# Flamingo block in fp32 on one core: weight centring and scaling moved from GpSimd to VectorE, keys and values taken ahead of the maxima

## The reference

```
x = x + tanh(g_xattn) * attention(layernorm(x), ctx)
x = x + tanh(g_ffn)   * experts(layernorm(x))

attention:  ln = LN(h); xq_t = fp8(clip(ln / in_scale_t))           t in q, qx, k, v
            q, qx, k = LN over D of ((xq_t * in_scale_t) @ W_t.T * w_scale_t), v likewise without LN
            kx, vx = split(ctx @ w_kv_x.T); kx = LN over D
            core = softmax(q k / sqrt(D)) v;  xout = softmax(qx kx / sqrt(D)) vx
            out = fp8(clip(cat(core, xout) / smooth)) @ wproj.T * scales
experts:    8 experts, top 2 of softmax(30 tanh(x @ w_gate / 30)), h = silu(x @ w1) * (x @ w3), out = h @ w2
```

## Time and profile before

| what | value |
| --- | --- |
| device time, median of 3 runs | 826.39 us |
| device time of the profiled execution | 827.05 us |
| its span, first to last instruction | 825.0 us |
| granted TensorE clock, mean | 0.96 |
| busy: PE, DVE, ACT, POOL | 84%, 62%, 61%, 60% |
| busy of a unit of the last group (16.76 us): PE, DVE, ACT, POOL | 16.03, 12.28, 13.48, 10.49 us |

### The profile page before, as it was taken

How to read it: one execution, slowest core, us unless ns; L and a number is a source line. 1 busy time by engine, 2 the same in 40 slices (tenths; PEclk the granted TensorE clock), 3 DMA queues, 4 the chain that set the end, 5 groups by cost and what they waited for, 6 DMA issues and landing times. The chain is left out here.

```text
span 825.0 us, 14882 instructions
## 1 busy us (share of the span) xinstructions
PE 691.2 (84%) x4662; PEld 593.5 (72%) x4663; DVE 512.5 (62%) x1148; ACT 502.0 (61%) x1861; POOL 495.2 (60%) x681
## 2 busy tenths in 40 slices
PE   0278899899989899998999998999875559999992
PEld 0267788888888888888888887889864426565662
DVE  5976767877777787777777767777776341211210
ACT  1567786887787788778778787778751112222220
POOL 4347687768867776886777687676542023444332
PEclk9999999999999999999999999999998559999997
DMA  5010110010010001001000100100000867532223
GB/s 183 27 51 1 40 39 1 1 53 27 1 52 27 1 2 52 26 1 52 27 1 2 52 26 2 52 2 1 1 1 2 269 191 248 131 51 41 48 32 70
DMA packets 35924, 38.90 MB, mean 47 GB/s; under 512 B 2720, under 2 KB 30752, under 8 KB 35840
## 3 DMA queue, kind: packets, MB, share of 16 engines
q1 hardware_dynamic: 31440, 32.02, 12.2%
q0 software_dynamic: 4416, 6.03, 4.5%
HBM read 32.67 MB, written 6.42 MB: 47 GB/s over the span
## 5 line engine op out<-in xcount | busy, mean ns | idle before, releaser
L796 POOL TENSOR_SCALAR probs<-probs,rsum 128x256 f32<-128x256 f32 x256 | 154.4, 614 | 75.9 <-DVE rsum L578 72.2
L405 ACT ACTIVATE probs<-s,nmax 128x256 f32<-128x256 f32 x256 | 122.0, 497 | 1.6 <-DVE nmax L573 1.6
L411 ACT CAST pt_hi<-t 128x512 fp32r<-128x512 f32 x128 | 75.8, 592 | 71.2 <-PE t L260 71.1
L419 ACT ACTIVATE qk<-t,head_w 128x512 f32<-128x512 f32 (+1 forms) x128 | 83.6, 682 | 45.3 <-PE t L272 45.3
L583 DVE TENSOR_TENSOR pt_lo<-t,pt_hi 128x512 fp32r<-128x512 f32 x128 | 87.6, 684 | 32.1 <-ACT pt_hi L411 31.7
L260 PE MATMUL t<-ident,probs 128*128 128x128 f32 x512 | 78.3, 275 | 17.3 <-POOL probs L796 16.5
L790 POOL TENSOR_TENSOR rstd<-rstd,half 128x6 f32<-128x6 f32 x64 | 87.7, 1371 | 5.3
L214 PE MATMUL pj_a<-w_ring,xq 128*128 128x256 f32 x496 | 75.0, 294 | 17.7 <-DVE w_ring L632 15.2
L573 DVE TENSOR_REDUCE nmax<-s 128x2 f32<-128x512 f32 x128 | 86.8, 679 | 0.0
L226 PE MATMUL pj_b<-w_ring,xq 128*128 128x128 f32 x496 | 68.9, 282 | 20.2 <-DVE v_lo L556 20.2
L1085 PE MATMUL h<-w_sb,xsT 128*128 x184 | 84.7, 604 | 0.6 <-ACT xsT L1192 0.5
(11 more groups left out here) (190 smaller groups left out, 1796.9 us busy)
## 6 DMA issues: line engine op xcount, KB each, us to landing
w_sb<-in_w SPq DMA_DIRECT2D x24, 512.0 KB, 5.2
spare<-in_wT SPq DMA_DIRECT2D x16, 256.0 KB, 2.9
wp_raw<-in_wpT SPq DMA_DIRECT2D x16, 256.0 KB, 2.9
spare<-in_wT SPq DMA_DIRECT2D x16, 128.0 KB, 3.1
spare<-in_wkvT SPq DMA_DIRECT2D x16, 128.0 KB, 3.1
acc<-in_x SPq DMA_DIRECT2D x1, 1024.0 KB, 5.9
start<-in_ctxT SPq DMA_DIRECT2D x1, 1024.0 KB, 7.2
spare<-in_x SPq DMA_DIRECT2D x1, 1024.0 KB, 5.4
```

The lines of the kernel that those rows point to most:

```text
L405: e = act.activation(probs[:, st, h * S:(h + 1) * S], s_bank[st][:, h * S:(h + 1) * S], ACT.Exp, bias=nmax[:, st, h:h + 1], accum_out=psum ...
L411: act.copy(pt_hi[:, :, st * P:(st + 1) * P], pt_bank[:].rearrange("p (n s) -> p n s", n=4)).then_inc(pthi_done, 1)
L419: m = act.activation(qk[:, at + c0:at + c0 + n], hd_bank[:, c0:c0 + n], ACT.Identity, scale=head_w[:, 2 * w:2 * w + 1], bias=head_w[:, 2 * ...
L796: m = pool.tensor_scalar(probs[:, st, c], probs[:, st, c], rsum[:, st, h:h + 1], 1.0, ALU.mult, ALU.mult)
```

## The change

POOL no longer scales and centres weights; DVE does both. The product of input scale and weight scale is written once into `w_scale`. `sum_weights(g, k)` now takes one half k, straight from the loaded weights, and makes the mean. `centre_weights(g, k, blocks)` subtracts the mean and multiplies by the scale in one small instruction for each block of 128 columns, 7 a half and 14 a group. They are spread over units: the sums of group g + 2 in b = 2 (one half at the start of the unit, one in its middle), the blocks of half 0 in b = 3 and those of half 1 in the b = 0 that follows (four at the start, three in the middle). For group 1 the sums and blocks lie in unit 0. ACT's casts and DVE's weights_lo lie in b = 0 and b = 1. `wp_hi` and `wp_lo` are cut in two halves, in b = 2 and b = 3. In the second half of a unit DVE takes normalise_kv(u+2, 0) ahead of both row_max, and quantise(u-1, 1) behind probs_lo.

```diff
@@ -437,8 +440,7 @@
 
-                if c % 2 == 0:
-                    act.wait_ge(w_centred, 2 * g + 1 + c // 2)
+                act.wait_ge(w_centred, 2 * g + 1 + c // 2)
                 if c == 0:
@@ -489,28 +491,33 @@
 
+            def prepare(g, b, place):
+
+                if g + 1 < G and b < 2:
+                    c = 2 * b + place if g > 0 else (b - 1) * 9 + 2 * place
+                    for n in ((c,) if g > 0 else (c, c + 1)):
+                        if 0 <= n < 4:
+                            weights_hi(g + 1, (g + 1) % 2, n)
+
             def step(g, par, b):
...
                 g1 = later(g, par, b, -1)[0]
-                prep = b == 1 and below(u + 4)
 
...
                     probs_hi(u - 1, 1, 0)
+                prepare(g, b, 0)
                 if below(u + 1):
...
                 exps(u, 0, 0)
-                if prep:
-                    weights_hi(g + 1, 1 - par, 0)
                 if above(u, 0):
...
                 exps(u, 0, 1)
-                if prep:
-                    weights_hi(g + 1, 1 - par, 1)
+                prepare(g, b, 1)
                 if above(u, 0):
@@ -518,15 +525,11 @@
                 probs_hi(u, 0, 1)
-                if prep:
-                    weights_hi(g + 1, 1 - par, 2)
                 exps(u, 1, 0)
...
                 exps(u, 1, 1)
-                if prep:
-                    weights_hi(g + 1, 1 - par, 3)
                 smooth(g, u, 0)
@@ -621,10 +624,24 @@
 
-            def sum_weights(g):
-                dve.wait_ge(w_scaled, g + 1)
-                dve.tensor_reduce(w_mean[:], w_raw[:, :, 0:NC_C * D].rearrange("p k (n d) -> p k n d", d=D), AX,
+            def sum_weights(g, k):
+                dve.wait_ge(w_loaded, 16 * W_DMAS * (g + 1))
+                dve.tensor_reduce(w_sum[:, k], w_raw[:, k, 0:NC_C * D].rearrange("p (n d) -> p n d", d=D), AX,
                                   ALU.add).then_inc(w_summed, 1)
+                dve.wait_ge(w_summed, KT * g + k + 1)
+                dve.tensor_scalar(w_mean[:, k], w_sum[:, k], 1.0 / D, None, ALU.mult).then_inc(w_meaned, 1)
+
+            def centre_weights(g, k, blocks):
+
+                dve.wait_ge(w_meaned, KT * g + k + 1)
+                for n in blocks:
+                    w = w_raw[:, k, n * D:(n + 1) * D]
+                    if n < NC_C:
+                        m = dve.tensor_scalar(w, w, w_mean[:, k, n:n + 1], w_scale[:, k, n:n + 1], ALU.subtract, ALU.mult)
+                    else:
+                        m = dve.tensor_scalar(w, w, w_scale[:, k, n:n + 1], None, ALU.mult)
+                if n == 7:
+                    m.then_inc(w_centred, 1)
 
@@ -635,6 +652,7 @@
             dve.memset(half[:], -0.5)
+            dve.memset(w_scale[:], 1.0).then_inc(ones_set, 1)
             dve.wait_ge(x_loaded, 16)
@@ -651,13 +669,22 @@
             dve.tensor_scalar(inv_smooth[:], inv_smooth[:], GRID, None, ALU.mult).then_inc(consts_ready, 1)
+            dve.wait_ge(ones_set, 1)
+            for i, blks in enumerate(((0, 1), (2, 3), (4,), (7,))):
+                for n in blks:
+                    m = dve.tensor_tensor(w_scale[:, :, n], col[:, C_INS + i * KT:C_INS + (i + 1) * KT],
+                                          col[:, C_SCAL + i:C_SCAL + i + 1].broadcast_to([P, KT]), ALU.mult)
+            m.then_inc(w_scales_ready, 1)
             dve.wait_ge(ctx_hi_done, 1)
...
                                   ALU.subtract, ALU.mult).then_inc(z_ready, 1)
-            sum_weights(0)
+            dve.wait_ge(w_scales_ready, 1)
+            for k in range(KT):
+                sum_weights(0, k)
+                centre_weights(0, k, (0, 1, 2, 3, 4, 5, 7))
             dve.wait_ge(consts_ready, 1)
@@ -705,11 +732,24 @@
 
+            def prepare(g, b, place):
+
+                if g == 0 and b == 0:
+                    centre_weights(1, place, (0, 1, 2, 3, 4, 5, 7))
+                if b == 2 and g + 2 < G:
+                    sum_weights(g + 2, place)
+                if b == 3 and g + 2 < G:
+                    centre_weights(g + 2, 0, ((0, 1, 2, 3), (4, 5, 7))[place])
+                if b == 0 and g > 0 and g + 1 < G:
+                    centre_weights(g + 1, 1, ((0, 1, 2, 3), (4, 5, 7))[place])
+
             def step(g, par, b):
...
                 bv, bh = (b + 2) % B, (b + 1) % B
-                prep = b == 1 and below(u + 4)
-
+                if u == 0:
+                    for k in range(KT):
+                        sum_weights(1, k)
+                prepare(g, b, 0)
                 if above(u, 0):
@@ -727,21 +767,22 @@
                     split_heads(u + 1, bh, 0)
-                if prep:
-                    weights_lo(g + 1, 1 - par, 0)
-                    weights_lo(g + 1, 1 - par, 1)
+                if g + 1 < G and b == 1:
+                    for c in ((0, 1) if g == 0 else (2,)):
+                        weights_lo(g + 1, 1 - par, c)
                 row_sum(u, 0, 1)
 
+                prepare(g, b, 1)
                 if below(u + 2):
...
                 probs_lo(u, 0, 0)
+                if below(u + 2):
+                    normalise_kv(u + 2, bv, 0)
                 row_max(u, 1, 0)
+                row_max(u, 1, 1)
+                probs_lo(u, 0, 1)
                 if above(u, 0):
                     quantise(u - 1, 1)
-                if below(u + 2):
-                    normalise_kv(u + 2, bv, 0)
-                row_max(u, 1, 1)
-                probs_lo(u, 0, 1)
                 row_sum(u, 1, 0)
@@ -749,13 +790,14 @@
                             x1_normalise(b - 3)
-                if b == 0 and below(u + 4):
-                    sum_weights(g + 1)
                 if below(u + 1):
                     split_heads(u + 1, bh, 1)
-                if prep:
-                    weights_lo(g + 1, 1 - par, 2)
-                    weights_lo(g + 1, 1 - par, 3)
+                if g + 1 < G and g > 0 and b == 0:
+                    for c in (0, 1):
+                        weights_lo(g + 1, 1 - par, c)
+                if g + 1 < G and b == 1:
+                    for c in ((2, 3) if g == 0 else (3,)):
+                        weights_lo(g + 1, 1 - par, c)
                 row_sum(u, 1, 1)
@@ -818,36 +860,22 @@
 
-            def scale_weights(g):
-
-                wait(w_loaded, 16 * W_DMAS * (g + 1))
-                for i, (blk, n) in enumerate(((0, 2), (2, 2), (4, 1), (7, 1))):
-                    for k in range(KT):
-                        w = w_raw[:, k, blk * D:(blk + n) * D]
-                        m = pool.tensor_scalar(w, w, col[:, C_INS + i * KT + k:C_INS + i * KT + k + 1],
-                                               col[:, C_SCAL + i:C_SCAL + i + 1], ALU.mult, ALU.mult)
-                m.then_inc(w_scaled, 1)
-
-            def centre_weights(g, k):
-
-                if k == 0:
-                    wait(w_summed, g + 1)
-                    pool.tensor_scalar(w_mean[:], w_mean[:], 1.0 / D, 1.0, ALU.mult, ALU.mult).then_inc(w_meaned, 1)
-                    wait(w_meaned, g + 1)
-                w = w_raw[:, k, 0:NC_C * D].rearrange("p (n d) -> p n d", d=D)
-                pool.tensor_tensor(w, w, w_mean[:, k, :].rearrange("p (n o) -> p n o", o=1)
-                                   .broadcast_to([P, NC_C, D]), ALU.subtract).then_inc(w_centred, 1)
-
-            def wp_hi(g, par):
-                wait(wp_loaded, 32 * (g + 1))
-                if above(g, 1):
-                    wait(out_done, 4 * (g - 1))
-                pool.tensor_scalar(wp_ring[:, par, 0], wp_raw[:], 1.0, 1.0, ALU.mult, ALU.mult).then_inc(wp_hi_done, 1)
-
-            def wp_lo(g, par):
-                wait(wp_hi_done, g + 1)
-                pool.tensor_tensor(wp_ring[:, par, 1], wp_raw[:], wp_ring[:, par, 0].bitcast(F32),
-                                   ALU.subtract).then_inc(wp_ready, 1)
+            def wp_hi(g, par, a):
+
+                if a == 0:
+                    wait(wp_loaded, 32 * (g + 1))
+                    if above(g, 1):
+                        wait(out_done, 4 * (g - 1))
+                n = slice(2 * a, 2 * a + 2)
+                pool.tensor_scalar(wp_ring[:, par, 0, n], wp_raw[:, n], 1.0, 1.0, ALU.mult, ALU.mult).then_inc(wp_hi_done, 1)
+
+            def wp_lo(g, par, a):
+                wait(wp_hi_done, 2 * g + a + 1)
+                n = slice(2 * a, 2 * a + 2)
+                m = pool.tensor_tensor(wp_ring[:, par, 1, n], wp_raw[:, n], wp_ring[:, par, 0, n].bitcast(F32),
+                                       ALU.subtract)
+                if a == 1:
+                    m.then_inc(wp_ready, 1)
 
@@ -867,11 +895,10 @@
             pool.wait_ge(cols_loaded, 32)
-            scale_weights(0)
-            for k in range(KT):
-                centre_weights(0, k)
-            wp_hi(0, 0)
-            wp_lo(0, 0)
+            for a in range(2):
+                wp_hi(0, 0, a)
+            for a in range(2):
+                wp_lo(0, 0, a)
             power(0, 0)
@@ -891,12 +918,8 @@
                 if prep:
```

(21 more changed lines are left out.)

## The result

| | before | after |
| --- | --- | --- |
| device time, median | 825.98 us (824.77 to 827.87, 4 runs) | 851.34 us (849.26 to 852.22, 4 runs) |
| ratio | | 1.029, 95% interval 1.027 to 1.032 |
| span of the profiled execution | 825.0 us | 848.5 us |
| granted TensorE clock, mean | 0.96 | 0.925 |
| four units of a middle group | 18.15, 18.30, 17.29, 17.58 us | 16.99, 17.54, 24.25, 16.59 us |

The change makes the kernel 2.9% slower. It was forecast slower, 841 us in a range of 825 to 856: the way is right, the size is short by 10 us.

The account below looks back on a forecast made before the run. PE sets the pace, so its waits count. On the profiled 827.05 us: groups 1 to 5 +14.0, group 0 +6.8, group 6 -6.0, group 7 -1.3, start 0; total +13.5, 840.5, given as 841, range 825 to 856.

Parts of the forecast that it names:

- Part 4: Start of b = 2, groups 0 to 5: sum_weights waits for the weight load; unit 25.0 us, 7.7 more.
- Part 1: DVE's second half of a unit: normalise_kv ahead of row_max and quantise ends the v_lo wait; 0.63 us gained a unit.
- Parts 2 and 3: Weight work from POOL to DVE: without any stall, b = 0, 1, 3 at 16.4, 16.3, 16.4 us, together 4.9 less.
- The blocks: DVE's 14 small operations a group, in b = 3 and b = 0: 0.24 us each, about 0.3 a unit exposed.
- Rival (d): First blocks of b = 0 and 3 wait out POOL's power, about 1.0 us in 13 units: 854 us, chance 0.10.
- Groups 1 to 5: Middle groups: 7.7 us more in b = 2 less 4.9 in the other units, five times, +14.0 us.
- Group 0: First group: unit 0 +2.5, unit 1 -2.2, b = 2 +7.7, a further -1.2; +6.8 us.
- Group 6: Group without a stall: -4.9 and -1.1, together -6.0 us.
- Group 7: Last group, where no weights are prepared: -1.3 us.
- Start: Before the units: DVE's centring +4.8 us, quantising no longer beside POOL's weight work -5.1; about zero, bounds -1 and +1.5.
- (b): All units: relief of 5.9 us a group outweighs the stall, clock stays up, b = 2 costs 5.3; 818 us, chance 0.20.
- (e): DVE's new order yields nothing as normalise_q or row_max becomes the wait: 29 x 0.63 more, 859 us, chance 0.07.

Follow-up runs that it names:

- e1: The changed kernel with both sums of group g+2 moved to the middle of unit b = 2, nothing else moved: 806.73 us, ratio 0.977 to the kernel before.
- e4: e1 with the old order of DVE's second half of a unit: 817.23 us, ratio 0.990 to the kernel before.
- e5: e1 with quantise back between the two maxima of the second half, normalise_kv still ahead of both: 808.26 us.

## Why the prediction was right, and where it was short

**Part 4, the stall: right.** The prediction had w_ready 6.5 us ahead of the landing, DVE idle for 6.4 and PE for 7.2, half clock behind it for 1.7, and 25.0 for the unit. Measured: DVE 6.54, PE 6.60, unit 24.25, and 1.8 for the clock by the filled stall. Taken out, the stall is worth 44.6 us in six groups, 7.4 each. The term that was too large is PE's idle time: 5.9 to 6.9, on average 6.3, for 7.2. PE was to arrive 1.8 us after w_ready, by a lead of 0.7 from part 1, and arrived 2.4 after it (249.73 and 247.33 in the rows above).

**Part 1, the new order: the step that failed.** It said that quantise "moves some 2.3 us back; POOL's widening follows it and is wanted by PE only at the unit's end", bounded the gain by 0 and 0.73 a unit and took 0.63. It asked who wants widen's result and not what is queued behind widen on POOL: scale_probs, power and, before the change, the centring. Alone the new order costs 4.9 us (1.0 in the profiled execution), outside the bounds; in units without weight work it gains 0.4 (16.76 to 16.34), where the 0.1 of new waiting that was allowed for came to about 0.3; and beside the moved weights, e1 against e4, it is worth 10.5 us instead of 18.

**Parts 2 and 3, the relief: right way, over-sized with part 1.** Units b = 0, 1 and 3 were to fall by 4.9 together and fell by 2.9, to 51.1. The largest miss is b = 1: 17.54 for 16.3. These rows of the changed kernel, from the end of b = 0 to the middle of b = 1, show what was not counted:

```profile
227.99 2.06 POOL L838 TENSOR_SCALAR probs<-probs,rsum 128x256 f32<-128x256 f32 x2
...
228.33 0.85 DVE L571 TENSOR_TENSOR qk_lo<-qk,qk_hi 128x512 fp32r<-128x512 f32 x1
229.11 1.48 DVE L649 TENSOR_TENSOR w_ring<-spare,w_ring 128x512 fp32r<-128x512 f32 x2
...
230.73 1.34 POOL L832 TENSOR_TENSOR rstd<-rstd,half 128x6 f32<-128x6 f32 x1
...
232.10 0.69 DVE L549 TENSOR_TENSOR start<-pj_a,rstd 128x512 f32<-128x512 f32 x1 [0.92 <-POOL rstd L832]
...
232.85 0.66 PE L275 MATMUL t<-ident,start 128*128 128x128 f32 x4 [0.66 <-DVE start L549]
...
236.60 2.24 POOL L838 TENSOR_SCALAR probs<-probs,rsum 128x256 f32<-128x256 f32 x2 [1.58 <-DVE rsum L581]
...
238.90 0.66 PE L263 MATMUL t<-ident,probs 128*128 128x128 f32 x4
```

The pair of scale_probs takes 2.06 where it otherwise takes 0.94. It runs beside three DVE instructions with two inputs in SBUF, and the trace as a whole shows the same: 66 pairs with no such neighbour took 0.93 to 1.10, 13 pairs with three took 2.06 to 2.31. POOL's power comes late by that, normalise_q of the next unit waits for it, and PE waits 0.66. Late quantise has pushed scale_probs there. Against the unit b = 1 of group 7 (16.30) b = 1 here is 1.24 longer: 0.4 of it arises at this wait, 0.4 by the middle of the unit, where the next stretched pair (2.24) ends as PE turns the probabilities, and 0.4 at the last turn_probs, behind a third pair of 2.06. So the two engines did hold each other up, but POOL paid for it, and not the new operations.

**The blocks.** Taken at 0.24, they measured 0.25. Rival (d), that they wait out POOL's power, falls: in the loop of the changed kernel 50 of the 84 that also centre ran wholly inside a power and took 0.33 to 0.35, as with POOL idle. Here the trace agrees with the row of before and not with the Trainium skill's rule (SBUF — State Buffer, "SBUF: two separate sides") that a GpSimd instruction which starts first holds the pair for its whole length, if these small operations are of the two-port kind that the rule names. The 2.06 above, beside DVE instructions with two SBUF inputs, agrees with what the same section says of these.

**The sum.** Groups 1 to 5: +19.6 for 14.0. Here two errors of opposite sign meet: the relief was 2.0 a group short, more than the 1.5 that the range allowed it, and b = 2 rose by 6.8 instead of 7.7, which gave 0.9 a group back. Without the second the time would have come out some 5 us higher, at the edge of the range, so there was luck in how well the range held. Group 0: +6.0 for 6.8, with unit 0 at +2.0 for 2.5. Group 6: -4.0 for -6.0. Group 7: +0.5 for -1.3, since its unit b = 2, which has no projections, rose from 15.44 to 16.43; the old order (15.46 in e4) and quantise in the middle (15.45 in e5) have it back, so that is the late quantise. Start: 56.04 for 55.99, the zero that was forecast out of +4.8 and -5.1; by the rows of the start they were +5.1 and -5.2, since the first quantising step begins at 27.35 for 22.23 and the first weights_lo at 35.46 for 35.57. What follows the units took 1.3 us more, 193.0 for 191.7, although nothing is changed there. The same stretch took 191.1 to 195.0 in the profiled executions of the ten kernels, which leave it alone too, so 1.3 us lies within its scatter. Together +23.5 of span.

**Rivals.** (b) fell, since the stall was exposed whole. Its relief of 5.9 a group was not reached either: with the stall out, in e1, units b = 0, 1 and 3 still fell by 2.9 only. (e) is partly true: normalise_q did become the wait, of 0.26 to 0.67 in the units without a stall, and of 0.3 alone where there is no weight work.

## What to carry to other kernels

A step that reads a freshly loaded single buffer belongs as far behind the buffer's release as the load takes, some 6.6 us here (247.33 to 253.98); put first in an engine's order, it makes every instruction behind it wait for a DMA. When an operation is pushed back, ask what is queued behind the instruction that waits for it on the next engine, and not only who wants its result. Two edits that are worth +5 and -9 us apart can be worth -20 together, so try the pair before dropping either.

## What the runs showed of the hardware that had not been expected

A GpSimd power on 128x6 (1.33 us) did not hold up VectorE's tensor_scalar inside it (0.33 to 0.35 us), while a tensor_scalar of GpSimd did (up to 1.03 for 0.29). One of those cases in the kernel before, DVE and POOL, the copy of wp_hi:

```profile
185.55 1.02 DVE L594 TENSOR_SCALAR y<-y 128x512 int16<-128x512 int16 x1
...
185.26 1.16 POOL L845 TENSOR_SCALAR wp_ring<-wp_raw 128x1024 fp32r<-128x1024 f32 x1
```

And more work can cost less time: 52 extra transposes in each of six stalls made the kernel 8.5 us faster, by keeping the granted clock at 1.00, where behind the stall it was 0.50.
